# Values' product behind visit 2 of the feed-forward blocks; opening, passage to the experts and first late group in another order

## The chip, the cores and the metric

The kernel runs on one core of a Trainium2 chip. The metric is the device time of one execution in microseconds (us), the median of the runs. PE is TensorE, DVE VectorE, ACT ScalarE, POOL GpSimd and SP the sync engine, which here only issues DMAs. "Landing" is the moment at which the engine that waits for a DMA can go on.

## The reference

Input x has 16 sequences of 512 tokens, 128 features. First a linear attention block with a causal mask and no softmax, then a normed residual, then a mixture of 8 experts beside a shared feed-forward, and a second normed residual:

```python
q = silu(x @ Wq); k = silu(x @ Wk); v = x @ Wv          # 16 heads of 8
q = concat([q*cos(theta*n), q*sin(theta*n)]); k likewise
energy = einsum('bhnd,bhmd->bhnm', q, k) * tril
out = einsum('bhnm,bhmd->bhnd', energy, v) @ Wo * sigmoid(x @ G1 @ G2)
x = layernorm(x + (layernorm(out) * gamma + beta))
logits = rmsnorm(x) @ router_w.T        # two best of 8 experts, by capacity 1280
routed = scatter_add(expert(x[dispatch]) * w)
shared = silu(x @ sg) * (x @ su) @ sd
x = layernorm(x + shared + routed)
```

## The kernel before

Five engines have their own hand-written program, and semaphores alone tie them together; the order of the lines in each program is the order of execution.

**Stage 1** (up to 510 us) walks over the 16 sequences, "blocks" b = -1 to 17. Block b holds the core of attention for sequence b (PE's `energies`, `state`, `from_states`, `attend`, in four visits c = 0 to 3; DVE's `mask` and `mask_state`), the front of sequence b+1 (`project`, `values_projected`, `keys_turned`), and the back of the sequences before (norms, routing, `dispatch` by POOL). Blocks 2 to 11 (`with_feed_forward`) also run one shared feed-forward: eight pairs of `shared_gate(f)` and `shared_up(f)` on PE, `shared_silu` and `hidden_hi` on ACT, `shared_hidden` and `hidden_lo` on DVE. The gate's product and the energies share a bank of PSUM: `energies(c)` waits until ACT has read the gate before (`gates_before`), and `shared_gate(3)` waits until DVE has masked visit 2's first half of energies (`v_mask`). In the order of before, PE runs in the middle of such a block: out of visit 1, gate 2, `values_projected(0)`, up 2, energies of visit 2, gate 3. `values_projected(0)` is six matmuls (L2288 to L2290); ACT's `values` reads them out with three activations, and stands before `hidden_hi(b, 2)`.

**Opening** (0 to 20 us): POOL makes constants, SP loads `theta`, x and weights, DVE makes the angles of the rotary table in a chain of dependent small steps (L1183 to L1202), ACT takes their sine, DVE forms the table and turns the first queries and keys.

**Passage** (510 to 557 us): two further shared feed-forwards, called RELOADED and AGAIN (`spread_pair`, `spread_silu`, `spread_hidden`, `spread_down`), are woven with the norm and routing of the last two sequences. Each sequence's rows go to the experts' table in eight indirect DMAs issued by POOL (`dispatch`, L627); dispatch 16 needs the slots that DVE works out in `slots(B, 0)`, dispatch 17 those of `slots(B + 1, 1)`. When all have landed, SP loads the first expert's rows, and PE turns them (L2382).

**Stage 2** (557 to 755 us) walks over the 8 experts, PE without a wait; POOL adds their rows to the sums in DRAM.

**Stage 3** (755 to 823 us) adds three late feed-forwards (g = 0, 1, 2) to the sums and norms 16 sums ("jobs"; FIRST_JOB is 0, 3, 9, 15). A job is loaded into one of six buffers, DVE takes statistics (`stats`, `spread`), POOL the reciprocal root, ACT norms it in place (`normed`, 4 activations), SP stores it. SP's queue holds, for job n: wait for the norm, store job n, wait until that store has completed, load job n+6 into the same buffer. `added` puts the feed-forward's result, which stands in bank UB, onto its job; the next group's first up (L1850 on `bank`) writes UB and waits for it.

```python
need(sp, m_o, 4 * (n + 1) - (2 if g == LATE else 0))
sp.dma_start(out_v[m], ac[:, n % NB]).then_inc(m_st[n % NB], 16)
load_sums(n + NB)
```

## Time and profile before

| what | us |
|---|---|
| median of 3 runs (823.49 to 828.65) | 825.48 |
| the profiled execution's own time | 824.92 |
| its span, first to last instruction | 822.9 |
| PE busy | 768.0 (93%) |
| DVE busy | 586.1 (71%) |
| POOL busy | 405.8 (49%) |
| ACT busy | 368.4 (45%) |
| share of PE in the chain that ended last | 77% |

The profile is of one execution. PE's busy time is that of pipelined matmuls, so 93% does not say that PE is at its peak; it says that PE seldom stands still. In block 4 one matmul of 128x512 starts about 0.23 us after the one before while its record is 0.39 us long, so lengths of a stretch are read from starts. An "idle before" in brackets behind a row names the time for which the engine had nothing to do, and who ended it.

### The profile page before, as it was taken

The numbers are of one execution on the slowest core, as the hardware profiler recorded it, in microseconds if no ns is written. First come the engines' busy times: TensorE is split into PE (matmuls) and PEld (weight loads), VectorE is DVE, ScalarE is ACT, GpSimd is POOL, SyncE is SP. The second block draws the span as 40 slices with busy tenths as digits, with TensorE's granted clock in tenths as the row PEclk, the third lists the DMA queues.
The fourth block names the chain that finished last, engine by engine and source line by source line (L and its number), as shares of the span: only waits on it lengthen the run. The fifth ranks groups of instructions, "written<-read, shape, count | busy, mean of one in ns | idle before, by whom it ended". The sixth has DMA issues, their size and how long they took to land.

```text
span 822.9 us, 30732 instructions
## 1 busy us (share of the span) xinstructions
PE 768.0 (93%) x12462; PEld 625.8 (76%) x12462; DVE 586.1 (71%) x1866; ACT 368.4 (45%) x802; POOL 405.8 (49%) x395
## 2 busy tenths in 40 slices
PE   5889999999999999999998898989999999999994
PEld 3667777777777777777776676768999988899884
DVE  7488898888888898898878988744444454544675
ACT  6425554646556464554633331223323333323584
POOL 5541242523335243332534554571677778876442
PEclk9999999999999999999999999999999999999998
DMA  4155233231423323232222212113443445433555
GB/s 146 47 174 179 80 91 82 64 98 48 99 76 78 89 57 96 58 88 76 69 73 63 61 33 67 46 58 128 98 86 45 89 98 105 71 50 43 128 148 145
DMA packets 71164, 70.56 MB, mean 86 GB/s; under 512 B 11444, under 2 KB 54251, under 8 KB 71025
## 3 DMA queue, kind: packets, MB, share of 16 engines
q1 hardware_dynamic: 54000, 52.33, 23.0%
q0 software_dynamic: 17024, 16.28, 11.0%
q8 instruction: 99, 1.62, 0.9%
q14 instruction: 41, 0.33, 0.1%
HBM read 23.99 MB, written 28.89 MB: 64 GB/s over the span
## 4 chain that ended last, share of the span: by engine, by line
PE 77%; DVE 11%; issue 4%; DMA 3%; POOL 2%; SPq 1%; ACT 1%; POOLq 0%; ACTq 0%; DVEq 0%
PE energy_banks L1932 6%; PE bank L1850 5%; PE energy_and_gate_banks L1850 5%; PE bank L1852 5%; PE bank L1851 5%; PE bank L2406 4%; PE energy_and_gate_banks L2406 4%; PE energy_and_gate_banks L1957 4%; PE energy_and_gate_banks L1852 3%; PE energy_and_gate_banks L1851 3%; PE bank L1891 3%; DVE EM L1242 3%; PE energy_banks L1850 3%; PE energy_banks L1852 3%; PE energy_banks L1851 3%
## 5 line engine op out<-in xcount | busy, mean ns | idle before, releaser
L627 POOL DMA_INDIRECT dispatched_rows<-x,slot x128 | 130.5, 1019 | 236.4 <-PE energy_banks L1932 142.8
L761 POOL DMA_INDIRECT summed_rows<-VP,goal_i x80 | 123.8, 1548 | 43.3 <-issue 22.7
L1119 ACT ACTIVATE sq<-energy_banks 128x512 f32<-128x512 f32 (+1 forms) x96 | 50.6, 527 | 120.2 <-PE energy_banks L1852 116.6
L832 ACT ACTIVATE sf<-energy_and_gate_banks 128x512 f32<-128x512 f32 x88 | 52.4, 596 | 70.5 <-PE energy_and_gate_banks L1852 69.8
L842 ACT ACTIVATE hidden_rounded<-sf 128x512 fp32r<-128x512 f32 x88 | 55.3, 628 | 52.4 <-DVE sf L1272 52.4
L1272 DVE TENSOR_TENSOR sf<-sf,bank 128x512 f32<-128x512 f32 x88 | 60.3, 685 | 18.3 <-PE bank L1852 16.8
L1932 PE MATMUL energy_banks<-EM,VP 64*32 64x64 f32 x4096 | 59.0, 227 | 2.2 <-issue 2.2
L1850 PE MATMUL energy_and_gate_banks<-xgT_hi,ws_hi 128*128 128x512 f32 x108 | 51.7, 479 | 9.9 <-DVE EM L1242 9.3
L1242 DVE TENSOR_TENSOR EM<-energy_and_gate_banks,causal 128x512 f32<-128x512 f32 x64 | 44.1, 688 | 20.1 <-PE energy_banks L1957 20.0
L1932 PEld LDWEIGHTS energy_banks<-EM,VP 64*32 64x32 f32 x4096 | 47.6, 106 | 5.4 <-issue 4.6
L1850 PE MATMUL bank<-xgT_hi,ws_hi 128*128 128x512 f32 x108 | 45.5, 421 | 3.6 <-DVE QM L1789 1.7
L1724 DVE TENSOR_TENSOR he<-sq,bank 128x512 f32<-128x512 f32 (+1 forms) x48 | 28.8, 599 | 27.1 <-PE bank L1852 22.3
L1957 PE MATMUL energy_and_gate_banks<-QM,KT 32*64 32x128 f32 x1024 | 43.9, 281 | 2.9 <-issue 2.2
L1957 PEld LDWEIGHTS energy_and_gate_banks<-QM,KT 32*64 32x64 f32 x1024 | 28.6, 132 | 22.7 <-issue 22.4
L1957 PE MATMUL energy_banks<-QM,KT 32*64 32x128 f32 x1024 | 44.3, 282 | 0.9 <-issue 0.9
L1242 DVE TENSOR_TENSOR EM<-energy_banks,causal 128x512 f32<-128x512 f32 x64 | 43.5, 680 | 0.0
L1852 PE MATMUL bank<-xgT_hi,ws_lo 128*128 128x512 f32 x108 | 42.7, 395 | 0.0
L1852 PE MATMUL energy_and_gate_banks<-xgT_hi,ws_lo 128*128 128x512 f32 x108 | 42.7, 395 | 0.0
L1851 PE MATMUL bank<-xgT_lo,ws_hi 128*128 128x512 f32 x108 | 42.6, 395 | 0.0
L1851 PE MATMUL energy_and_gate_banks<-xgT_lo,ws_hi 128*128 128x512 f32 x108 | 42.5, 394 | 0.0
L1977 PE MATMUL bank<-VP,Kt 64*32 64x32 f32 x1792 | 40.6, 198 | 1.2 <-ACT Kt L891 0.8
L1724 DVE TENSOR_TENSOR he<-sq,energy_and_gate_banks 128x512 f32<-128x512 f32 (+1 forms) x48 | 28.8, 599 | 16.5 <-PE energy_and_gate_banks L1852 12.6
(256 smaller groups left out, 2189.4 us busy)
## 6 DMA issues: line engine op xcount, KB each, us to landing
QM<-QT SPq DMA_DIRECT2D x248, 32.0 KB
dispatched_rows<-empty POOLq DMA_DIRECT2D x8, 655.0 KB, 4.2
QM<-dispatched_rows SPq DMA_DIRECT2D x8, 655.0 KB, 5.6
QT<-sq SPq DMA_DIRECT2D x40, 128.0 KB, 2.8
KT<-sq SPq DMA_DIRECT2D x40, 128.0 KB
xin<-in_x SPq DMA_DIRECT2D x16, 256.0 KB, 2.9
QM<-summed_rows SPq DMA_DIRECT2D x16, 256.0 KB, 2.8
out_x<-QM SPq DMA_DIRECT2D x16, 256.0 KB, 3.2
```

The costliest lines, as they stand in the source:

```text
L627: g.indirect_dma_start(out=xg_d, out_offset=bass.IndirectOffsetOnAxis(ap=slot[:, n % 2, j:j + 1], axis=0), in_=x1[:, n % 2, j % NC, :], in ...
L761: g.indirect_dma_start(out=sum_d, out_offset=bass.IndirectOffsetOnAxis(ap=goal_i[:, par, t:t + 1], axis=0), in_=ye[:, par, t, :], in_offse ...
L842: a.activation(hs_hi[:, f], sf[:, n % SF], ACT.Copy).then_inc(a_hh, 1)
L1242: v.tensor_tensor(EM[:, c % 2, i].rearrange("p (r h) n -> p r h n", r=2), (EG2, EB2)[i][:, :, 0:4 * T].rearrange("p r (h n) -> p r h n", h=4),
L1272: v.tensor_tensor(sf[:, n % SF], sf[:, n % SF], UB[:], ALU.mult).then_inc(v_h, 1)
L1724: v.tensor_tensor(he[:, hp, f, 0:w], sq[:, f % 2, 0:w], EB[2 + f % 2][:, 0:w], ALU.mult).then_inc(e_h, 1)
L1850: t.matmul(dst, w_hi, x_hi, start=True, stop=False)
L1851: t.matmul(dst, w_hi, x_lo, start=False, stop=False)
L1852: return t.matmul(dst, w_lo, x_hi, start=False, stop=True)
L1932: ins = t.matmul(AV2[32 * j:32 * j + 32, s, cols], VP[keys, par, c, 32 * h:32 * h + 32], EM[keys, c % 2, h % 8 // 4, h % 4 // 2 * 4 + h // ...
L1957: ins = t.matmul((EG2, EB2)[r // 2][T * s:T * (s + 1), r % 2, 2 * T * t2:2 * T * (t2 + 1)], KT[rows, par, t2, P * c + T * s:P * c + T * (s ...
L2406: ins = t.matmul((OB, SBK)[hp][:, P * c:P * (c + 1)], he[:, hp, f, P * c:P * (c + 1)], wd[:, par, f], start=(f == 0), stop=(f == 3))
```

## The change

- **Blocks 2 to 11.** PE runs `values_projected(0)` behind up 2 and visit 2's energies instead of between gate 2 and up 2. ACT runs `hidden_hi(b, 2)` before `values(f, fp, 0)`.
- **Opening.** The second half of `theta` is loaded from ACT's queue instead of SP's; POOL makes `bits` before `ident`; `bits` holds 0.25 in place of 1.0, so that one reduction gives the phase, and a multiplication falls away; two memsets of DVE stand ahead of its wait for POOL.
- **Passage.** DVE: `add_input(B)`, `second_moments(B)`, `mean_square(B)`, `slots(B, 0)` and `scale_x1(B, 1)` stand earlier, `shared_add(RELOADED)` behind the routing of B+1. PE: `down_back` before `positions(B)`; `positions(B + 1)` and parts of `spread_down(RELOADED)` change places. ACT: the copy of x1T before that of `xhi`.
- **Stage 3.** The loads of sums go 0, 3, 1, 2, 4, 5 instead of 0 to 5. DVE runs `added` for job 3 right behind the statistics of job 0, not behind those of jobs 0, 1 and 2. ACT norms only job 0 in group 0; job 1 and job 2 are normed between the silus of group 1.

```diff
@@ -384,7 +384,6 @@
...
             sp.dma_start(theta_s[0::2], theta_v[0]).then_inc(ld_t, 16)
-            sp.dma_start(theta_s[1::2], theta_v[1]).then_inc(ld_t, 16)
             sp.dma_start(xin[:, 0], x_v[0]).then_inc(ld_x, 16)
...
@@ -509,7 +508,7 @@
...
             sp.wait_ge(e_sc[1], 16 * CT * E // 2)
-            for n in range(NB):
+            for n in (0, FIRST_JOB[1], 1, 2, 4, 5):
                 load_sums(n)
...
@@ -528,18 +527,18 @@
...
             g = nc.gpsimd
-            g.memset(ident[:], 0.0).then_inc(c_id, 1)
-            gp.wait_ge(c_id, 1)
-            g.affine_select(out=ident[:], in_=ident[:], compare_op=ALU.not_equal, fill=1.0, base=0,
-                            pattern=[[-1, P]], channel_multiplier=1).then_inc(c_id, 1)
             g.memset(zeros[:], 0.0).then_inc(c_pool, 1)
...
             for n in (0, P // 4):
-                g.affine_select(out=bits[:, n:n + P // 4], in_=bits[:, n:n + P // 4], compare_op=ALU.not_equal, fill=1.0, base=-2 * n,
+                g.affine_select(out=bits[:, n:n + P // 4], in_=bits[:, n:n + P // 4], compare_op=ALU.not_equal, fill=0.25, base=-2 * n,
                                 pattern=[[-2, P // 4]], channel_multiplier=1).then_inc(c_pool, 1)
+            g.memset(ident[:], 0.0).then_inc(c_id, 1)
+            gp.wait_ge(c_id, 1)
+            g.affine_select(out=ident[:], in_=ident[:], compare_op=ALU.not_equal, fill=1.0, base=0,
+                            pattern=[[-1, P]], channel_multiplier=1).then_inc(c_id, 1)
 
...
@@ -778,6 +777,7 @@
...
             a = nc.scalar
+            act.dma_start(theta_s[1::2], theta.rearrange("(h t d) i -> t h d i", t=2, d=HD)[1]).then_inc(ld_t, 16)
             act.wait_ge(c_pool, 1)
...
@@ -962,8 +962,8 @@
...
                     shared_silu(b, 2)
+                    hidden_hi(b, 2)
                     values(f, fp, 0)
-                    hidden_hi(b, 2)
                     shared_silu(b, 3)
...
@@ -1083,11 +1083,11 @@
...
             spread_silu(RELOADED, 7)
+            act.wait_ge(pe_x1T, B)
+            a.activation(x1T[:], PB[1][:], ACT.Copy).then_inc(a_x1T, 1)
             act.wait_ge(pe_again, 2)
...
             a.activation(xhi[:, 1], OB[:], ACT.Copy).then_inc(a_x1h, 1)
-            act.wait_ge(pe_x1T, B)
-            a.activation(x1T[:], PB[1][:], ACT.Copy).then_inc(a_x1T, 1)
             second_choice(B + 1, 1)
...
@@ -1155,15 +1155,17 @@
...
                     shared_silu(f)
-                    if g > 0 and f in (0, 1):
+                    if g == 1:
+                        normed(n - 2 + f // 2, (2 * (f % 2), 2 * (f % 2) + 1))
+                    if g > 1 and f in (0, 1):
                         normed(n - 1, (2 * f, 2 * f + 1))
-                    if g > 0 and f in (3, 4):
+                    if g > 1 and f in (3, 4):
                         normed(n, (2 * f - 6, 2 * f - 5))
-                    if g > 0 and f in (5, 6):
+                    if g > 1 and f in (5, 6):
                         normed(n + 1, (2 * f - 10, 2 * f - 9))
...
                     split_late(r + 1, g + 2)
-                for k in (range(n, n + 2) if g == 0 else range(n + 2, n + (5 if g < LATE - 1 else 6))):
+                for k in (range(n, n + 1) if g == 0 else range(n + 2, n + (5 if g < LATE - 1 else 6))):
                     normed(k)
...
@@ -1179,11 +1181,10 @@
...
                 dve.wait_ge(c_dve, n_c[0])
-            dve.wait_ge(c_pool, 5)
-            link(v.tensor_reduce(cosine[:], bits[:], AX.X, ALU.add))
-            link(v.tensor_scalar(phase[:], cosine[:], 0.25, None, ALU.mult))
             for i in (0, 1):
                 link(v.memset(shift_by[:, i], 0.25 * i))
+            dve.wait_ge(c_pool, 5)
+            link(v.tensor_reduce(phase[:], bits[:], AX.X, ALU.add))
             link(v.tensor_scalar(shift_by[:, :, 0:2 * COARSE], shift_by[:, :, 0:2 * COARSE], phase[:, 0:1], None, ALU.add))
...
@@ -1655,30 +1656,30 @@
...
             centre(B)
+            add_input(B)
             spread_hidden(RELOADED, 2)
+            second_moments(B)
             copy_logits(B)
             two_best(B)
-            add_input(B)
             spread_hidden(RELOADED, 3)
             choices(B, 0)
+            mean_square(B)
             spread_hidden(RELOADED, 4)
-            second_moments(B)
             spread_hidden(RELOADED, 5)
-            mean_square(B)
             read_positions(B)
+            slots(B, 0)
             spread_hidden(RELOADED, 6)
-            slots(B, 0)
+            scale_x1(B, 1)
             spread_hidden(RELOADED, 7)
-            scale_x1(B, 1)
             dve.wait_ge(m_x1[0], 16)
...
             two_best(B + 1)
-            shared_add(RELOADED, x1t[:, 1])
             choices(B + 1, 1)
...
             slots(B + 1, 1)
+            shared_add(RELOADED, x1t[:, 1])
             for f in range(8):
...
@@ -1819,7 +1820,7 @@
...
                     return
-                if g > 0:
+                if g > 1:
                     added(r - 1, n)
...
@@ -1837,6 +1838,8 @@
...
                     spread(k)
+                    if g == 0 and k == n:
+                        added(r, FIRST_JOB[1])
             stage3(dve, group)
...
@@ -2133,9 +2136,9 @@
...
                     shared_gate(2)
-                    values_projected(0)
                     shared_up(2)
                     energies_and_state(2)
+                    values_projected(0)
                     shared_pair(3)
...
@@ -2347,18 +2350,18 @@
...
             spread_pair(RELOADED, 5)
+            down_back(SPARE, PB[0])
             positions(B)
-            down_back(SPARE, PB[0])
             spread_pair(RELOADED, 6)
...
             turn_again(1, x1[:, 0])
-            spread_down(RELOADED, (0, 1))
             turn_x1(B + 1, 1)
-            spread_down(RELOADED, (2,))
+            spread_down(RELOADED, (0,))
             logits(B + 1)
-            spread_down(RELOADED, (3,))
+            spread_down(RELOADED, (1,))
+            positions(B + 1)
+            spread_down(RELOADED, (2, 3))
             spread_pair(AGAIN, 0)
-            positions(B + 1)
             for f in range(1, 8):
...
             spread_down(AGAIN, (0, 1))
```

## Rows read from the trace of the kernel before

**Rows 1.** PE's waits in the whole run: us in total, times, longest
```profile
PE energy_and_gate_banks L1850 <- DVE EM L1242: 9.3, 13, 1.4
```

**Rows 2.** Timeline, block 4, PE: start us, us, what, idle before
```profile
144.35 0.28 PE L2288 MATMUL bank<-we_hi,xgT_hi 128*128 128x256 f32 x1
...
145.06 0.39 PE L1850 MATMUL bank<-xgT_hi,ws_hi 128*128 128x512 f32 x1
...
145.84 0.33 PE L1957 MATMUL energy_and_gate_banks<-QM,KT 32*64 32x128 f32 x2
...
147.43 0.50 PE L1850 MATMUL energy_and_gate_banks<-xgT_hi,ws_hi 128*128 128x512 f32 x1 [0.63 <-DVE EM L1242]
```

**Rows 3.** Timeline, block 4, DVE
```profile
145.09 0.68 DVE L1223 TENSOR_TENSOR QT<-QT,table 128x512 f32<-128x512 f32 x1
...
146.02 0.69 DVE L1272 TENSOR_TENSOR sf<-sf,bank 128x512 f32<-128x512 f32 x1 [0.24 <-PE bank L1852]
...
146.68 0.69 DVE L1242 TENSOR_TENSOR EM<-energy_and_gate_banks,causal 128x512 f32<-128x512 f32 x1
...
147.29 0.68 DVE L1242 TENSOR_TENSOR EM<-energy_banks,causal 128x512 f32<-128x512 f32 x1
```

**Rows 4.** Timeline, block 4, ACT
```profile
144.55 0.60 ACT L832 ACTIVATE sf<-energy_and_gate_banks 128x512 f32<-128x512 f32 x1
...
146.74 0.63 ACT L842 ACTIVATE hidden_rounded<-sf 128x512 fp32r<-128x512 f32 x1 [0.77 <-DVE sf L1272]
...
148.43 0.60 ACT L832 ACTIVATE sf<-energy_and_gate_banks 128x512 f32<-128x512 f32 x1 [1.05 <-PE energy_and_gate_banks L1852]
```

**Rows 5.** Timeline of the opening, SP's queue and DVE
```profile
0.80 0.84 SPq L386 DMA_DIRECT2D theta_s<-in_theta  x1
...
1.70 0.64 SPq L387 DMA_DIRECT2D theta_s<-in_theta  x1
...
3.69 0.23 DVE L1190 TENSOR_SCALAR SM<-y,theta_s 128x16 f32<-128x16 f32 x1
```

**Rows 6.** Timeline of the passage, POOL
```profile
518.18 1.05 POOL L600 TENSOR_TENSOR rs<-ve,minus_half 128x4 f32<-128x4 f32 x1
...
529.75 1.03 POOL L627 DMA_INDIRECT dispatched_rows<-x,slot  x1 [1.07 <-DVE slot L1407]
...
532.98 0.97 POOL L627 DMA_INDIRECT dispatched_rows<-x,slot  x1 [2.20 <-issue]
```

**Rows 7.** Timeline of the passage, DVE
```profile
520.08 0.19 DVE L1360 COPY lg<-bank 128x32 f32<-128x32 f32 x1 [0.62 <-PE bank L2267]
```

**Rows 8.** Timeline of the passage, PE
```profile
556.99 1.97 PE L2382 MATMUL bank<-ident,QM 128*128 128x128 f32 x8 [4.75 <-DMA QM<-dispatched_rows]
```

**Rows 9.** Chain that ended last, inside the first expert
```profile
568.92 0.87 PE bank L2382 x8
```

**Rows 10.** Stretches: bounds, length, PE busy (instructions), PEclk, DMA share, GB/s
```profile
57.00:58.00 1.00, 0.00 (x0) 1.00 0.38 120
...
59.00:60.00 1.00, 0.92 (x59) 0.50 0.26 59
```

**Rows 11.** Timeline of the last stage, SP's queue
```profile
774.61 0.39 SPq L521 DMA_DIRECT2D out_x<-QM  x1
...
776.93 0.32 SPq L503 DMA_DIRECT2D QM<-summed_rows  x1
...
777.29 0.51 SPq L521 DMA_DIRECT2D out_x<-QM  x1
...
810.53 0.32 SPq L503 DMA_DIRECT2D QM<-summed_rows  x1
```

**Rows 12.** Timeline of the last stage, ACT
```profile
772.94 3.19 ACT L1145 ACTIVATE QM<-QM,shift,rs 128x128 f32<-128x128 f32 x8 [5.70 <-POOL shift L774]
```

**Rows 13.** Timeline of the last stage, DVE
```profile
771.41 0.86 DVE L1760 BATCH_NORM_STATS2 st<-QM 128x6 f32<-128x128 f32 x4
```

**Rows 14.** Timeline of the last stage, PE
```profile
775.36 0.47 PE L1850 MATMUL bank<-xgT_hi,ws_hi 128*128 128x512 f32 x1 [1.57 <-DVE QM L1789]
```

## The prediction

> **What bounds the kernel now.** I read the page first: PE is busy for 93% of the span and holds 77% of the chain that ended last, so what doesn't shorten PE's path, or the few stretches in which PE waits, brings nothing. Then PE's waits: the largest entry by far is the shared gate behind DVE's mask, 9.3 us in 13 places [rows 1]. Ten of the 13 are one per block 2 to 11. The timeline of block 4 shows the place: energies of visit 2 start at 145.84, gate 3 could follow the state's product but stands for 0.63 and starts at 147.43 [rows 2], once DVE has run the hidden product at 146.02 and the mask's first half at 146.68 [rows 3]. Then the three places outside the blocks where the chain leaves PE: the opening, a chain of small DVE steps behind the load of theta [rows 5]; the passage, where POOL issues dispatches one after another while PE ends up idle for 4.75 [rows 6, 8]; and the last stage, where SP's queue is a chain of its own: from 776.93 to 810.53 it loads nine times (jobs 7 to 15 after job 6) and each step is "store, wait for its completion, load": 33.6 / 9 = 3.73 us each [rows 11].
>
> **Blocks 2 to 11.** Nothing is added or removed, six matmuls move. Their length is 145.06 - 144.35 = 0.71 [rows 2]. Without them up 2 runs at 144.35 and visit 2's energies could start 0.71 earlier, at 145.13. They need the gate's bank, which ACT reads from 144.55 to 145.15 [rows 4]; with a hand-over of about 0.06 (an estimate: gate 3 starts 0.06 after the mask's record ends, 146.68 + 0.69 against 147.43) [rows 2, 3] they start at 145.21, so 0.08 of the move is lost here. The values then fill the place in which PE stood. DVE now decides. It began its turn at 145.09 and starts operations of this shape 0.61 apart when it has work (146.68 to 147.29), so the hidden product starts at 145.70 instead of 146.02, where it had waited 0.24 for up 2, and the mask at 146.31 instead of 146.68 [rows 3]. Its input, the energies, started 0.63 earlier, so is there. Gate 3 starts 0.37 earlier, at 147.06. PE is ready for it at 147.43 - 0.63 = 146.80 plus 0.08 and a refill of the pipeline behind the values, about 0.1 (estimate: a first matmul's record is 0.50, a following one's 0.39), thus 146.98 [rows 2, 3]: a rest of 0.1 remains. Bounds: at least DVE's idle of 0.24, at most the whole wait of 0.63. I take 0.37, **10 x 0.37 = 3.7 us**; the bounds are 2.4 and 6.3.
>
> What is queued behind: on ACT, `hidden_hi(2)` now stands before the three activations of `values`. Before, these ran between silu 2's end at 145.15 and 146.74 - 0.77 = 145.97, so 0.82 [rows 4]. Now PE's values end about 147.0 and ACT is free at 147.8. The next silu can start when gate 3 is done, 148.43 - 0.37 = 148.06. This cover is 0.25 per block; beyond it silu 3, then gate 4, come late. DVE's order is unchanged; POOL's dispatches hang on PE's counts and move with them; SP's queue isn't touched. The product's bank is needed again only when the keys are turned, eight microseconds later.
>
> **Opening.** The first angle step, at 3.69, needs both halves of theta [rows 5]. The second was issued at 1.70, behind the first at 0.80; from ACT's queue it goes out beside the first, 0.9 earlier. SP's later loads (x, wqk) also move up by the 0.64 which that issue took. The DVE steps before it shrink by a reduction-and-scale hand-over, and POOL starts `bits` earlier, so theta is what is late next. ACT's table load comes behind its DMA issue; it is covered, since ACT's next needed work is the copy of wqk. The steps behind it, 3.69 to the table, keep their lengths in the sum. Gain between 0.6 (only SP's issue time of 0.64 comes off) and 1.5 (the 0.9 and the 0.64 add up where x, too, is waited for). I take **0.9**.
>
> **Passage.** The end of POOL's queue counts: dispatch 16's first DMA starts at 529.75, released by the slots, the second at 532.98 after 2.20 without work, and 14 more behind it [rows 6]; the rows land for PE at 556.99 [rows 8]. Earlier slots move all of it. In DVE's order, three things change ahead of `slots(B, 0)`: hidden 6 steps behind it (0.61, as above [rows 3]); the idle of 0.62 in front of the logits' copy [rows 7] is filled by `add_input`; and `add_input` now waits for POOL's root, which ends at 518.18 + 1.05 = 519.23 [rows 6]. By DVE's order that wait opens about 0.4 us. Gain 0.61 + 0.62 - 0.4 = **0.8**; bounds 0 (the root comes later) and 1.2 (it costs nothing). Behind that wait stand hidden 2 and 3 and so PE's ups 4 and 5, about 1 us late; and `spread_down(RELOADED)` behind `positions(B + 1)` pushes PE's end another microsecond or so. That is covered by PE's idle of 4.75 [rows 8], of which I expect about 2 to be left. Without that cover each microsecond would count in full. Slots of B+1 get earlier and POOL reaches dispatch 17 late, so nothing is gained there.
>
> **The clock at the passage's end.** In this run the eight transposes at 556.99 take 1.97 [rows 8], the same eight inside the first expert 0.87 [rows 9], and two products of the shared down follow, also slow; PE had stood for 4.75 us before. If the clock stays at 2.4 GHz the transposes give 1.1, and the downs perhaps 0.7 (an estimate: the same stretch again over what is left of the slow time). But the granted clock also fell to 0.50, that is 1.2 GHz, around 59, after an idle of only some 2 us of which 57 to 58 is a part [rows 10]; so I don't count it. The Trainium skill ("TensorE: Matmul & The Clock Gate", section "Why this matters for your kernels") advises against long idle gaps between bursts of matmuls, and by it the shorter pause would keep the clock up; the trace agrees only for the long gap, and shows a short one that cost it too.
>
> **Stage 3.** The gain aimed at is PE's wait of 1.57 in front of the group's first up [rows 14]: `added` can now run when the down product is done: PE was ready for that up at 775.36 - 1.57 = 773.8, behind a gate of about 0.7, so at 773.1. But PE has no place in what ends last here; SP's chain has. Store 0 goes at 774.61, its completion allows load 6 at 776.93, 2.32 later, then store 1 at 777.29 [rows 11]. Before, ACT had normed jobs 0 and 1 in one run, 772.94 to 776.13, 3.19 for eight activations [rows 12], so store 1 was ready. Now ACT norms job 0, then waits for gate 0's silu; and job 1's statistics stand on DVE behind `added` (0.7), from about 773.8 instead of 771.41 [rows 13], 2.4 later. Its norm can begin about 2.4 behind 774.5, at 776.9, needs 1.6 plus a silu of 0.5 between its halves: done near 779.0. Store 1 goes 1.75 late. It then runs alone, without load 6 beside it; store 0, alone, took 2.32 against a usual step of 3.73 - 0.36 = 3.4, so some 0.8 to 1 comes back. The rest stays on the chain to load 15 at 810.53, nine steps on [rows 11]. Loss between 0 (ACT is quicker) and 2.0; I take **0.9**.
>
> **Sum.** -3.7 - 0.9 - 0.8 + 0.9 = -4.5 us. Against the profiled execution: 822.9 of span becomes 818.4, and with the 2.0 around it 820.4. That execution lies 0.56 under the median of the runs, 825.48, on which I put the forecast: **821.0 us**.
>
> **Rivals.**
> - *The wait goes whole.* DVE's hand-over proves quicker and all 0.63 goes in ten blocks: 10 x 0.26 = 2.6 more, 818.4. For it: only 0.24 of idle lies in front of DVE; against it: the same, since the turn at 145.09 isn't moved. Chance 0.12.
> - *The clock stays up at the experts' start*, by the mechanism above: a further 1.8, 819.2. Chance 0.17.
> - *The change does not do what it says in the blocks*: the wait moves from gate 3 to the energies, because silu 2 sits on their bank. Only opening, passage and stage 3 are left: -0.9 - 0.8 + 0.9, 824.7. Against it: silu 2 ends at 145.15, 0.02 after the energies' earliest new start [rows 2, 4]. Chance 0.12.
> - *Slower.* ACT's values come between gate 3 and silu 3: gate 4 waits for silu 3. It decides from 0.25 + 0.37 = 0.62 us of lateness per block; if PE's values and their copies run 0.8 late, the block grows by 0.18, ten times, and with the other -0.8 the time is 826.5. At 0.7 late it is level with before. Chance 0.07.
>
> The forecast itself has 0.52. The range takes in the 0.12 and 0.17 below and the 0.12 above, with bounds of the terms: 817.0 to 825.0. Measurements here tell about 1% from no change, 8.3 us, so faster by over 1% means under 817.2; only the whole wait together with the clock and the long opening step gets there: 0.08. Slower by over 1% needs several of these to go wrong at once: 0.03. Within: 0.89.
>
> **What would show it.** PE's wait for the mask at gate 3 should fall from 0.63 to 0.1 to 0.3 per block, the block's period by 0.37, and a wait of at most 0.1 appear before visit 2's energies. The first angle step should start near 2.8. Dispatch 16 should start 0.8 earlier relative to the last block, PE's pause before the first expert should be near 2. SP's store 1 should come 4 us or more behind store 0 (2.68 before), and the span from store 0 to the end should grow by about 0.9, though PE's wait of 1.57 is gone. The forecast is wrong if ACT's silu 3 starts behind `values` and not behind gate 3, if the block's period doesn't move, or if store 1 isn't late.

## The result

The changed kernel takes 820.52 us (median of 20 runs, 816.84 to 825.40); the kernel before, on the same chips, 826.62 us (20 runs, 823.16 to 830.30). The ratio is 0.9927, 95% interval 0.9908 to 0.9947, thus 6.0 us less (4.4 to 7.6). The forecast was 821.0 us in a range of 817.0 to 825.0, and "within 1%". The profiled execution of the changed kernel has a span of 819.0 us, 3.9 under that of before. Line numbers in it are those of before plus 3 on PE (the gate is L1853), plus 1 on DVE, minus 1 on POOL and SP.

| | before | after |
|---|---|---|
| median of the runs, us | 826.62 | 820.52 |
| span of the profiled execution, us | 822.9 | 819.0 |
| PE's wait at the gate for DVE's mask, us (times) | 9.3 (13) | 2.6 (3) |
| period of blocks 4 to 10 (logits to logits), us | 35.23 | 34.96 |
| PE's pause ahead of the experts, us | 4.75 | 2.49 |
| loads of the last stage, first to last, us | 43.18 | 43.02 |

PE's waits of the whole run (us in total, times, longest) have the line of [rows 1] no longer at their head:

```profile
PE energy_and_gate_banks L1853 <- DVE EM L1243: 2.6, 3, 1.4
...
PE energy_and_gate_banks L1960 <- ACT sf L832: 0.4, 1, 0.4
```

The ten waits in blocks 2 to 11 (1.00 us in block 2, 0.63 in the others) are gone; the three that are left stand behind the blocks with a feed-forward. The second line is new: visit 2's energies wait once, in block 2, for ACT to have read their bank.

Block 4 in the timelines of PE, DVE and ACT (start, us, what, idle before it), which answer to [rows 2, 3, 4]:

```profile
144.92 0.33 PE L1960 MATMUL energy_and_gate_banks<-QM,KT 32*64 32x128 f32 x2
...
145.80 0.39 PE L2291 MATMUL bank<-we_hi,xgT_hi 128*128 128x256 f32 x1
...
146.26 0.38 PE L2291 MATMUL bank<-we_hi,xgT_hi 128*128 128x256 f32 x1
...
146.72 0.45 PE L1853 MATMUL energy_and_gate_banks<-xgT_hi,ws_hi 128*128 128x512 f32 x1
...
147.24 0.39 PE L1855 MATMUL energy_and_gate_banks<-xgT_hi,ws_lo 128*128 128x512 f32 x1
...
145.34 0.68 DVE L1273 TENSOR_TENSOR sf<-sf,bank 128x512 f32<-128x512 f32 x1
145.94 0.68 DVE L1243 TENSOR_TENSOR EM<-energy_and_gate_banks,causal 128x512 f32<-128x512 f32 x1
...
144.18 0.60 ACT L832 ACTIVATE sf<-energy_and_gate_banks 128x512 f32<-128x512 f32 x1
146.05 0.63 ACT L842 ACTIVATE hidden_rounded<-sf 128x512 fp32r<-128x512 f32 x1 [1.28 <-DVE sf L1273]
146.92 0.45 ACT L819 ACTIVATE VP<-bank 128x128 f32<-128x128 f32 x2 [0.24 <-PE bank L2293]
147.25 0.39 ACT L823 ACTIVATE th<-bank 128x256 f32<-128x256 f32 x1
147.67 0.60 ACT L832 ACTIVATE sf<-energy_and_gate_banks 128x512 f32<-128x512 f32 x1
```

PE goes from the energies (144.92) through the state's product to the values (145.80) and the gate (146.72) without a wait. DVE has no idle ahead of the hidden product at 145.34. ACT's silu 3 (147.67) still starts when gate 3 is done, 0.04 behind the record of its last matmul (147.24 + 0.39). It was the same 0.04 in the kernel before, where that silu starts at 148.43 [rows 4]:

```profile
148.00 0.39 PE L1852 MATMUL energy_and_gate_banks<-xgT_hi,ws_lo 128*128 128x512 f32 x1
```

What is new is that the values' tanh now stands close ahead of it, so that the idle of 1.05 [rows 4] is used up. The values take 0.92 us (145.80 to 146.72) instead of 0.71 [rows 2]: their first matmul now has a record of 0.39, and so has the fourth.

The opening, ACT's queue and DVE, against [rows 5]. The first block is the changed kernel, the second the kernel before:

```profile
0.80 1.21 ACTq L780 DMA_DIRECT2D theta_s<-in_theta  x1
...
3.15 0.23 DVE L1191 TENSOR_SCALAR SM<-y,theta_s 128x16 f32<-128x16 f32 x1 [0.68 <-DMA theta_s<-in_theta]
...
5.37 1.15 DVE L1201 SCALAR_TENSOR_TENSOR SM<-SM 128x192 f32<-128x192 f32 x3
6.55 1.34 DVE L1202 SCALAR_TENSOR_TENSOR SM<-SM 128x192 f32<-128x192 f32 x1
```

```profile
3.34 0.28 DVE L1187 TENSOR_SCALAR SM<-SM,phase 128x64 f32<-128x64 f32 x1
...
6.03 2.24 DVE L1200 SCALAR_TENSOR_TENSOR SM<-SM 128x192 f32<-128x192 f32 x3
8.30 0.36 DVE L1201 SCALAR_TENSOR_TENSOR SM<-SM 128x192 f32<-128x192 f32 x1
```

The second half of theta is issued at once, but the issue takes 1.21 us on ACT's queue, and the first angle step starts 0.54 earlier, not 0.9. In the kernel before no engine waited for theta: the step at 3.69 followed DVE's own step at 3.34 without idle. In the changed kernel DVE is ready 0.68 us ahead of it, and theta ends last. Of the 0.54, 0.38 is left where the table is written (9.81 to 9.43). The five steps ahead of that take 3.48 us together here (1.15 for three, then 1.34 and 0.99) and 3.20 in the kernel before (2.24, 0.36 and 0.60); in both a long one runs beside POOL's `we_lo` (6.75 to 8.05 before, 6.34 to 7.67 after), only it is not the same step. That POOL's work lengthens it is not shown. And in block 2 nothing is left of the gain. DVE turns the queries there behind their transfer; the first line is the kernel before, the second the changed one:

```profile
72.08 0.69 DVE L1223 TENSOR_TENSOR QT<-QT,table 128x512 f32<-128x512 f32 x1 [0.43 <-DMA QT<-sq]
```

```profile
72.04 0.69 DVE L1224 TENSOR_TENSOR QT<-QT,table 128x512 f32<-128x512 f32 x1 [0.89 <-DMA QT<-sq]
```

The passage on POOL, DVE and PE, against [rows 6, 7, 8]:

```profile
515.69 1.53 POOL L599 TENSOR_TENSOR rs<-ve,minus_half 128x4 f32<-128x4 f32 x1
...
527.09 1.03 POOL L626 DMA_INDIRECT dispatched_rows<-x,slot  x1 [1.68 <-DVE slot L1408]
530.32 0.97 POOL L626 DMA_INDIRECT dispatched_rows<-x,slot  x1 [2.19 <-issue]
...
517.42 1.14 DVE L1338 SCALAR_TENSOR_TENSOR s<-wv,rs,xb 128x128 f32<-128x128 f32 x4 [1.10 <-POOL rs L599]
...
554.76 1.09 PE L2385 MATMUL bank<-ident,QM 128*128 128x128 f32 x8 [2.49 <-DMA QM<-dispatched_rows]
...
559.40 0.47 PE L1853 MATMUL energy_banks<-xgT_hi,we_hi 128*128 128x512 f32 x1
```

The wait of `add_input` for POOL's root is there (1.10 instead of the 0.4 of the forecast), the 2.19 us ahead of the second dispatch too. PE's pause is 2.49 instead of 4.75, and the eight turns of the first rows take 1.09 instead of 1.97.

The last stage, SP's queue, against [rows 11]:

```profile
770.90 0.39 SPq L520 DMA_DIRECT2D out_x<-QM  x1
773.93 0.32 SPq L502 DMA_DIRECT2D QM<-summed_rows  x1
775.15 0.39 SPq L520 DMA_DIRECT2D out_x<-QM  x1
777.56 0.32 SPq L502 DMA_DIRECT2D QM<-summed_rows  x1
...
806.68 0.32 SPq L502 DMA_DIRECT2D QM<-summed_rows  x1
```

Store 1 comes 4.25 us behind store 0 (2.68 before), as forecast. From store 0 to load 15 there are 35.78 us, against 810.53 - 774.61 = 35.92 before [rows 11]: the 0.9 did not come.

**How the runs scatter.** The runs of one kernel differ by up to 9 us, and the clock explains most of it. The granted clock falls from 1.0 to 0.50 (from 2.4 to 1.2 GHz), mostly for 3.4 us and for up to 13.7 us, at places that change from run to run. In the profile of before it fell at 58.5, 471.5 and 556.8, in that of after at 59.2, 421.0 and 444.9. In all 14 profiles there is one more fall behind PE's last matmul (816.2 in before, 810.2 in after), where PE has nothing left to slow down. Of 239 runs of these kernels the record lists span and mean clock: with one level for each kernel, the span is 5.3 us longer for each 0.01 of mean clock that is missing, and scatters by only 1.2 us around that. A fall ahead of the experts costs about 1.5 us (measured below), so that the ratios of the runs have intervals of 0.2 to 0.3%, as much as each part of this change brings. What a part did is therefore read from distances inside the traces, and the ratio stands beside it.

### The profile page after: what moved, and what is told of

It reads as the page before. It is cut to its first block, busy times and chain, and to the rows that moved or that the text cites. A ratio compares the mean times of both kernels' runs of the same rounds, so it can differ in the third digit from the quotient of the medians.

```text
span 819.0 us, 30731 instructions
## 1 busy us (share of the span) xinstructions
PE 771.5 (94%) x12462; PEld 627.2 (77%) x12462; DVE 583.9 (71%) x1865; ACT 368.2 (45%) x802; POOL 415.7 (51%) x395
## 3 DMA queue, kind: packets, MB, share of 16 engines
q0 software_dynamic: 17024, 16.28, 11.0%
## 4 chain that ended last, share of the span: by engine, by line
PE 78%; DVE 10%; issue 4%; DMA 3%; SPq 2%; POOL 2%; ACT 1%; POOLq 0%; DVEq 0%; ACTq 0%
PE energy_banks L1935 5%; PE bank L1853 5%; PE energy_and_gate_banks L1853 5%; PE bank L1855 5%; PE bank L1854 5%; PE energy_and_gate_banks L2409 4%; PE bank L2409 4%; PE energy_and_gate_banks L1960 4%; PE energy_and_gate_banks L1855 3%; PE energy_and_gate_banks L1854 3%; PE bank L1894 3%; PE energy_banks L1853 3%; PE energy_banks L1855 3%; PE energy_banks L1854 3%; PE bank L1895 2%
## 5 line engine op out<-in xcount | busy, mean ns | idle before, releaser
L626 POOL DMA_INDIRECT dispatched_rows<-x,slot x128 | 140.0, 1093 | 224.5 <-PE energy_banks L1935 132.4
L1935 PE MATMUL energy_banks<-EM,VP 64*32 64x64 f32 x4096 | 59.1, 225 | 1.1 <-issue 1.1
L1853 PE MATMUL energy_and_gate_banks<-xgT_hi,ws_hi 128*128 128x512 f32 x108 | 52.1, 482 | 3.4 <-DVE EM L1243 2.6
L1853 PE MATMUL bank<-xgT_hi,ws_hi 128*128 128x512 f32 x108 | 45.9, 425 | 3.7 <-DVE sf L1273 1.4
L1853 PE MATMUL bank<-xgT_hi,we_hi 128*128 128x512 f32 (+1 forms) x92 | 37.5, 408 | 3.7 <-DVE xgT_lo L1205 3.0
```

The lines of the kernel that those rows point to most:

```text
L626: g.indirect_dma_start(out=xg_d, out_offset=bass.IndirectOffsetOnAxis(ap=slot[:, n % 2, j:j + 1], axis=0), in_=x1[:, n % 2, j % NC, :], in ...
L1853: t.matmul(dst, w_hi, x_hi, start=True, stop=False)
L1935: ins = t.matmul(AV2[32 * j:32 * j + 32, s, cols], VP[keys, par, c, 32 * h:32 * h + 32], EM[keys, c % 2, h % 8 // 4, h % 4 // 2 * 4 + h // ...
```

## The experiments

Each part was first made alone on the kernel before. The distances used below are in us, from one profiled execution of each kernel. A: logits of block 4 to logits of block 11 (135.75 to 382.37 in before), over seven; the expectations count the logits from the first that is there, so what they call blocks 3 and 10 is this distance, their "block 0" is block 2 of the kernel (65.04), their "block 1" and "block 2" are blocks 3 and 4 where logits are meant. B: the third dispatch ahead of POOL's root to dispatch 16 (514.59 to 529.75 in before). C: PE's pause ahead of the first rows. D: start of the rows' turns to the first expert's gate. E: first to last load of the last stage.

| kernel | A | B | C | D | E |
|---|---|---|---|---|---|
| before | 35.23 | 15.16 | 4.75 | 6.19 | 43.18 |
| blocks alone | 34.96 | 15.17 | 4.76 | 6.12 | 42.87 |
| opening alone | 35.26 | 15.12 | 4.62 | 6.09 | 43.18 |
| passage alone | 35.26 | 14.54 | 2.52 | 6.27 | 43.19 |
| last stage alone | 35.25 | 15.17 | 4.73 | 6.91 | 43.37 |
| blocks, ACT's order old | 35.04 | 15.15 | 4.65 | 6.25 | 43.17 |
| blocks, ACT's values cut | 34.97 | 15.11 | 4.72 | 6.28 | 42.76 |
| after | 34.96 | 15.01 | 2.49 | 4.64 | 43.02 |
| after, stores late | 34.97 | 14.53 | 1.98 | 6.27 | 42.65 |
| after, matmuls at 35.0 | 34.98 | 15.29 | 1.05 | 4.64 | 43.42 |
| after, pause of block 2 filled | 34.99 | 14.52 | 1.86 | 4.64 | 42.91 |
| after, down ahead of the rows | 34.95 | 14.52 | 0.48 | 2.85 | 43.15 |
| after, three edits | 34.95 | 14.52 | 0.15 | 2.85 | 43.59 |
| before, experts' pause filled | 35.27 | 15.17 | 2.02 | 4.64 | 42.37 |

**Blocks alone.** The edit is that of the diff in `with_feed_forward` on PE and ACT.

```diff
                     shared_gate(2)
-                    values_projected(0)
                     shared_up(2)
                     energies_and_state(2)
+                    values_projected(0)
```

> The kernel before with the edit of the blocks alone: the values' six matmuls behind visit 2's energies on PE, and ACT's hidden_hi(2) ahead of its values. From the profile of after, the block's period between the logits of blocks 3 and 10 fell from 35.22 to 34.96 us. My theory: this comes from the edit, so the same period here, 34.96, and ten blocks give 10 x 0.27 = 2.7 us, a ratio of 0.9967 to before. The prediction's size, 0.37 per block, would be a period of 34.85, 3.7 us, 0.9955. Rival: the blocks also gain through what the passage does to the clock or to the queues, then the period would be above 35.0. The clock at the experts' start is not touched by the edit: PE's pause before the first expert stays near 4.75 us and a drop of the granted clock near 556 stays.

Ratio 0.9954 (0.9927 to 0.9980). A is 34.96, 0.27 under before, as in the changed kernel: the gain of the blocks comes from this edit and from nothing else. PE's costliest lines over the seven blocks from the logits of block 4, before and then blocks alone (busy us, mean ns of one | idle ahead of them, and what ended it):

```profile
L1850 PE MATMUL energy_and_gate_banks<-xgT_hi,ws_hi 128*128 128x512 f32 x56 | 27.6, 492 | 4.5 <-DVE EM L1242 4.4
L1932 PE MATMUL energy_banks<-EM,VP 64*32 64x64 f32 x1741 | 24.4, 226 | 0.0
```

```profile
L1850 PE MATMUL energy_and_gate_banks<-xgT_hi,ws_hi 128*128 128x512 f32 x56 | 27.5, 492 | 0.1
L1932 PE MATMUL energy_banks<-EM,VP 64*32 64x64 f32 x1799 | 25.8, 225 | 0.0
```

All 4.4 us of waiting (0.63 times seven) are gone, and 1.92 us (0.27 times seven) of time is gained; against the other kernels without the edit, whose A is 35.25 to 35.27, it is 0.29 to 0.31 a block. Relative to the logits ahead of it, on the mean over the seven blocks, gate 3 starts 0.39 earlier (11.66 to 11.28) and gate 4 0.38 earlier, which is the step of the forecast; the gate behind that is only 0.29 earlier (16.28 to 15.99), and so is the rest of the block. Between the two stands the attention product of 64 matmuls, which takes 0.88 in before and 0.97 here. That is nearly the whole of what is lost; why the product grows isn't shown.

At the same mean clock and on the same chip, the runs of this kernel are 3.1 us (2.2 to 4.0) shorter than those of before: the one part of the four that the runs alone show clear of the clock.

**Opening alone.** The four hunks of the diff that touch the first steps of SP, POOL, ACT and DVE; its core:

```diff
-            sp.dma_start(theta_s[1::2], theta_v[1]).then_inc(ld_t, 16)
...
+            act.dma_start(theta_s[1::2], theta.rearrange("(h t d) i -> t h d i", t=2, d=HD)[1]).then_inc(ld_t, 16)
```

> The kernel before with the edit of the opening alone. In the profile of after the first angle step starts at 3.15 instead of 3.69, the logits of block 0 start 0.50 earlier, but in block 2 DVE's turn of the keys starts at 72.04 behind the transfer of the queries, against 72.08 before. My theory: the gain is swallowed there: the same turn starts at 72.0 to 72.1 here, and what is left behind block 2 is 0 to 0.1 us, a ratio of 0.9999 to 1.0000. Rival one: it is the order of the values in block 2, not the transfer, which cost that block its gain; then 0.4 to 0.5 us stay to the end (0.9994). Rival two: the prediction's 0.9 us (0.9989). The ratio's interval is near 0.001 wide, so the logits' starts decide between the first two.

Ratio 1.0003 (0.9975 to 1.0030). The first logits come at 63.64, 1.4 earlier than in the profile of before. That does not say that the edit gave 1.4: two kernels without it have theirs at 63.68 and 63.50 (ACT's order put back, the experts' pause filled). In these three the clock had not fallen ahead of the logits, as it had in before. DVE then stands 1.90 us for the queries:

```profile
72.16 0.69 DVE L1222 TENSOR_TENSOR QT<-QT,table 128x512 f32<-128x512 f32 x1 [1.90 <-DMA QT<-sq]
```

In eight of the nine other profiles in which DVE waited for this transfer, kernels with and without the opening's edit, the turn starts between 71.8 and 72.4 (in the ninth, ACT's values cut, at 73.05). So what the opening gains is swallowed here, and the edit brings nothing that these runs can show.

**Passage alone.** The three hunks of ACT, DVE and PE at the end of stage 1; what counts for dispatch 16 is DVE's:

```diff
             centre(B)
+            add_input(B)
             spread_hidden(RELOADED, 2)
+            second_moments(B)
...
             read_positions(B)
+            slots(B, 0)
             spread_hidden(RELOADED, 6)
-            slots(B, 0)
```

> The kernel before with the edit of the passage alone. In the profile of after, dispatch 16 gained only 0.1 to 0.15 us relative to the start of the passage (0.8 had been predicted), since add_input waits 1.10 us for POOL's root. My theory: the same here, 0.1 to 0.2, but PE's pause before the first expert is about 2.5 us instead of 4.75, no drop of the granted clock follows, and the eight transposes of the first rows take about 1.1 us instead of 1.97: together 1.5 us, so the time falls by 1.6 us, ratio 0.998. Rival: the clock at that place has nothing to do with the pause (it hangs on the time since the last drop, or on chance); then this run has the drop still, and the gain is 0.1 to 0.2 us, ratio 1.000.

Ratio 0.9970 (0.9943 to 0.9998), 2.5 us, of which most comes with the clock: the mean clock of these runs is 0.9898 against 0.9865 for before on the same chip, and at the same clock 0.5 us is left, which 0.9 either way can't tell from nothing. B falls by 0.62, where I expected 0.1 to 0.2 by the profile of after. The difference is POOL's root: 1.07 us here and 1.53 in the profile of after, and `add_input` waits 0.59 here and 1.10 there. Among the seven profiles with the passage's edit, the five with a root of 1.05 to 1.07 have B at 14.52 to 14.54, the two with 1.53 and 1.54 have 15.01 and 15.29. So the forecast's 0.8 was 0.6, and the profile of after had shown less of it than there is. The clock did not behave as I had expected either: the pause is 2.52, but the clock fell at 560.7, 0.6 us into the turns, and D is 6.27, as with the long pause.

**Last stage alone.** The four hunks of SP, ACT and DVE in stage 3; DVE's:

```diff
                     stats(k)
                     spread(k)
+                    if g == 0 and k == n:
+                        added(r, FIRST_JOB[1])
```

> The kernel before with the edit of the last stage alone. In the profile of after, store 1 came 4.25 us behind store 0 instead of 2.68, but the chain to load 15 was 0.14 us shorter than before, because one later step of 4.4 us before was 3.6 there. My theory: that long step was no part of the edit, and a late store 1 is given back by store 0 being quick (its completion 3.0 behind it when alone, not 3.7): the net is 0 to 0.3 us of loss, ratio 1.0000 to 1.0004. Rival one, the prediction: a loss of 0.9 us, 1.0011. Rival two: the edit removes the long step (other order, other fetches) and gains 0.5 to 1 us, 0.9990; then load 15 is reached over 0.5 us earlier behind store 0 than in a run of before, and store 6 to load 12 takes 3.6 us.

Ratio 0.9990 (0.9965 to 1.0015). Store 1 comes 4.18 us behind store 0, load 7 is 6.89 behind store 0 where before had 5.86, so 1.0 late; and E is 43.37, 0.19 over before. Over all profiles E is 42.96 on average in the seven without this edit (42.37 to 43.19) and 43.16 in the seven with it (42.65 to 43.59). The loss is 0.2 us, less than E scatters. What gave the rest back in these two is above all the step from load 11 to load 12: 4.76 us in before, 4.15 and 4.17 in opening alone and passage alone, but 3.98 in after and 3.58 here. Over all 14 profiles this step takes 3.74 to 4.76 us in the seven in which two transfers of instructions fall into it, and 3.48 to 3.85 in the seven with one. Two fall into it in four of seven kernels without the edit and in three of seven with it, after among these, so that it is not the edit which moves the chain out of their way. What does hold over all profiles: the eight steps behind load 7 take 28.79 to 29.35 us with the edit and 29.18 to 30.06 without, 0.6 less on the mean. Why isn't shown.

**ACT's order, put back.** Blocks alone, but `hidden_hi(b, 2)` behind `values(f, fp, 0)` again on ACT.

```diff
                     shared_silu(b, 2)
-                    hidden_hi(b, 2)
                     values(f, fp, 0)
+                    hidden_hi(b, 2)
                     shared_silu(b, 3)
```

> The kernel before with half of the blocks' edit: PE's six matmuls of the values stand behind visit 2's energies, but ACT keeps its old order, so hidden_hi(2) stands behind the three activations of the values. In the run with both halves (e1_blocks), block 4 showed PE's values ending at about 147.14, ACT's three activations from 147.17 to 147.9, silu 3 at 148.00, and gate 4 at 148.65, 0.05 us behind silu 3's end. My theory: here hidden_hi(2), some 0.5 us on ACT's path, is pushed in front of silu 3, silu 3 and gate 4 come 0.5 us late, and the block's period between the logits of blocks 3 and 10 is 34.96 + 0.5 = about 35.45, worse than before's 35.22: the time is 2.3 us above before, ratio 1.003. Rival, the cover of the prediction (0.25 us of idle ahead of silu 3, and a decision point of 0.62 us): only 0.5 - 0.25 = 0.25 is lost, period 35.2, ratio 1.000.

Ratio 0.9965 (0.9940 to 0.9990). Gate 4 does wait for silu 3 now. Waits of PE between 100 and 385 us:

```profile
PE energy_and_gate_banks L1850 <- ACT sf L832: 2.1, 8, 0.4
```

ACT in block 4:

```profile
148.23 0.39 ACT L823 ACTIVATE th<-bank 128x256 f32<-128x256 f32 x1
148.50 0.65 ACT L842 ACTIVATE hidden_rounded<-sf 128x512 fp32r<-128x512 f32 x1
149.02 0.60 ACT L832 ACTIVATE sf<-energy_and_gate_banks 128x512 f32<-128x512 f32 x1
```

The wait is 0.26 per block (0.41 in block 4, where silu 3 comes 0.37 later behind the logits than with both halves), half of what I expected. It is what the rival says, 0.5 less a cover of 0.25: ACT starts its next operation 0.27 behind the start of the values' tanh, and in the changed kernel silu 3 starts 0.42 to 0.57 behind it, 0.50 on the mean. That leaves ACT a cover of 0.24. But A is 35.04, only 0.08 more than with both halves: gate 4 is 0.27 late on the mean, the gate behind it only 0.06. The half edit still gains 0.2 per block. So the slower rival was far away: lateness beyond the cover does reach gate 4, but most of it is taken back behind.

**ACT's values cut in two.** Blocks alone, each of the three activations in two of half the width; the tanh:

```diff
+                if i == 0 and 3 <= f <= 12:
+                    a.activation(dst[:, 0:1], src[:, 0:1], ACT.Tanh, scale=0.5)
+                    a.activation(dst[:, 1:2], src[:, 1:2], ACT.Tanh, scale=0.5).then_inc(a_th, 1)
+                    return
                 a.activation(dst, src, ACT.Tanh, scale=0.5).then_inc(a_th, 1)
```

> The kernel before with the edit of the blocks, and in blocks 2 to 11 ACT's three activations of the first half of the values (two copies, one tanh) are cut into six of half the width. Nothing else changes, so only ACT's time between the values and silu 3 grows, by an estimated 0.35 to 0.5 us (three more starts; two copies of 128x128 start 0.33 us before the tanh, about 0.16 apart). This doubles the cost on which the slower rival of the prediction hangs. My theory: ACT has no cover left (silu 3 at 148.00 in block 4 of e1_blocks, no idle ahead of it), and gate 4 follows silu 3's end, so the whole of it shows: period 35.35 to 35.45, ratio to before 1.001 to 1.002, which turns a gain of 0.27 per block into a small loss. Rival, the prediction's cover of 0.25 us: period 35.1 to 35.2, ratio 0.998 to 1.000.

Ratio 0.9941 (0.9919 to 0.9964), A 34.97. The edit costs ACT less than I had expected. The four halves of the copies take 0.43 us from the first start to the tanh, the two copies had taken 0.33; the halves of the tanh start 0.16 apart, where the whole one had taken 0.27 to the next start. So ACT's work grows by about 0.15 us (an estimate from these starts) and not by 0.35 to 0.5. That is inside the cover of 0.24: silu 3 starts 0.03 or 0.04 behind gate 3's last matmul in six of the seven blocks and 0.09 behind it in the seventh, and the period doesn't move. My theory, that ACT has no cover left, is refuted by it.

**Two stores of empty rows later.** On the changed kernel, in POOL's part of block 2:

```diff
                     need(gp, pe_E, 8 * b + 2)
-                    fill(4 * b - 4)
...
                     need(gp, pe_av, 4 * b + 2)
+                    if b == 2:
+                        fill(4 * b - 4)
+                        fill(4 * b - 3)
                     fill(4 * b - 2)
```

> The changed kernel, with two of POOL's eight stores of empty rows (655 KB each, issued at 63.76 and 65.02, beside the transfer of the queries for block 2) issued about 12 us later, behind visit 2's attention product. In the profile of the changed kernel DVE stood 0.89 us for that transfer, until 72.04, and the same turn started at 72.04 to 72.4 in four profiles, whether the opening ended early or late. My theory: the stores share the transfer engines with the queries and set that time; here the turn starts by 71.2 (when DVE is ready) and blocks 1 and 2 end 0.8 us earlier: logits of block 1 at 99.6 to 99.9 where the clock fell as in the profile of the changed kernel (100.41), ratio to before lower by 0.001 than the changed kernel's own 0.9927. Rival: the transfer is bound by its own small packets or by its own issue, the stores do not matter, and the turn starts at 72.0 again, no gain.

Ratio 0.9928 (0.9905 to 0.9951). The turn of the queries (in block 2, for block 3) starts without a wait:

```profile
70.37 0.68 DVE L1228 TENSOR_TENSOR QT<-QT,table 128x512 f32<-128x512 f32 x1
```

That is 1.7 us earlier than in after, though the clock fell at 59.1 as there (59.2), and the logits of block 4 come at 133.92, 1.46 earlier; 0.7 of this was there at the first logits already (63.84 against 64.54). Against the kernel with the pause of block 2 filled (below), which has its first logits at 63.86 and waits 1.8 for the queries, block 4's come 1.7 earlier (135.62 there). DMA between 63 and 72 us, after and then this kernel:

```profile
DMA packets 1622, 2.55 MB, mean 283 GB/s; under 512 B 155, under 2 KB 1179, under 8 KB 1619
dispatched_rows<-empty POOLq DMA_DIRECT2D x2, 655.0 KB
```

```profile
DMA packets 1441, 1.36 MB, mean 151 GB/s; under 512 B 156, under 2 KB 1180, under 8 KB 1438
```

The two stores were half of what the DMA engines moved while the queries were under way. This is shown for the transfer, by one profile against the ten that waited; why the first logits were already 0.7 earlier is not. The ratio of the runs, 0.9928 against the changed kernel's 0.9927, can't tell 1.7 us.

**Five matmuls, misplaced.** On the changed kernel, in `first_blocks`:

```diff
+                    if b == 1:
+                        for _ in range(5):
+                            t.matmul(UB[:], wqk_hi[:, 0:P], wqk_hi[:, 0:512], start=True, stop=True)
                     states_and_out(0)
```

> The changed kernel, with five matmuls of 512 columns (1.2 us, result unused) on PE behind the turn of the input in block 1, where PE pauses for 2 us (56.1 to 58.1 in the profile of before). The granted clock fell to 0.50 shortly behind that pause in four of six profiles (58.5, 59.2, 59.9 us; later, at 65.8 and 77.3, in two; in one it did not fall), for 3.4 to 13.7 us. My theory: the pause brings the clock down, and with it filled the clock stays at 1.0 until the blocks have passed; at 0.50 a stretch takes up to twice its time, so this saves 1.5 us for a drop of 3.4 us and more for a longer one: about 2 us on the median, ratio to before 0.990 to 0.991, and the highest of the runs come down. Rival: the clock falls for another reason (chance, or the load of the transfers), the drop is there at 58 to 60 all the same, and the ratio stays 0.993.

Ratio 0.9926 (0.9904 to 0.9948). They ran at 35.0, a block early, where PE has no pause, and the pause of 1.95 ahead of 58.12 was untouched. The clock fell at 46.1, 59.8 and 517.2. It tells nothing on the pause.

**Five matmuls in the pause of block 2.** The same in `with_feed_forward`:

```diff
                     if b == 2:
                         input_turned()
+                        for _ in range(5):
+                            t.matmul(UB[:], wqk_hi[:, 0:P], wqk_hi[:, 0:512], start=True, stop=True)
```

> The changed kernel with five matmuls of 512 columns, result unused, now in the pause itself: behind the turn of the input in block 2, ahead of a pause that lasted 1.2 to 2.0 us in eight profiles (56.1 to 58.1 in that of before). In e9_fill_pause the same five stood one block too early, at 35.0, where PE has no pause; they ran there for 1.0 us, and the clock still fell at 59.8. My theory: PE's pause of 2 us has to do with the fall of the clock at 58.5 to 59.9 (six of eight profiles without a fall at another place before it), and with 1.2 us of it filled no fall comes before 66: blocks 1 and 2 end 1.0 to 1.7 us earlier. Rival: the fall comes all the same between 58 and 60, so that the pause isn't the cause.

Ratio 0.9910 (0.9884 to 0.9937). The pause went from 2 to 0.53 us and the clock did not fall before 808, behind PE's last matmul; but in the next kernel, without the matmuls and with a pause of 1.72, it did not fall either, and in the one behind it, with them, it fell at 52.1 and 65.7. For pauses of this length the question stays open.

**A quarter of the shared down ahead of the first rows.** On the changed kernel:

```diff
-            spread_down(AGAIN, (0, 1))
+            spread_down(AGAIN, (0, 1, 2))
...
                     turn_rows(0, 0, (0, 1))
-                    spread_down(AGAIN, (2,))
-                    turn_rows(0, 0, (2,))
                     spread_down(AGAIN, (3,))
+                    turn_rows(0, 0, (2,))
```

> The changed kernel, with one product moved at the experts' start. In its profile PE pauses for 2.49 us for the first rows (until 554.76), turns them, and then runs a quarter of the shared down (16 matmuls, 1.8 us, 555.69 to 557.48) before the last turn, another quarter, and the first expert's gate at 559.40. Here that quarter stands ahead of the pause. My theory: it fills 1.8 of the 2.5 us with work that had stood behind, so the first expert's gate comes 1.7 to 1.8 us earlier behind the rows' turn (2.8 us instead of 4.64 behind its start), because DVE's and ACT's parts of the rows are done by 557.4, and the clock stays at 1.0 there; the time falls by 1.7 us against the changed kernel, ratio to before about 0.9905 against 0.9927. Rival: POOL's split of the weights or the transfer of the rows ends last, or the product in the pause comes late itself, and the gate starts at the same distance as before.

Ratio 0.9918 (0.9885 to 0.9950). D is 2.85 instead of 4.64, as expected; PE pauses for 0.48 us:

```profile
552.33 1.10 PE L2385 MATMUL bank<-ident,QM 128*128 128x128 f32 x8 [0.48 <-DMA QM<-dispatched_rows]
...
555.18 0.48 PE L1853 MATMUL energy_banks<-xgT_hi,we_hi 128*128 128x512 f32 x1
```

**All three.** The diffs of the stores, of the pause of block 2 and of the shared down together.

> The changed kernel with three edits together: the two late stores of empty rows of e7_fill_late (there the turn of the queries started at 70.4 instead of 72.04, and block 2's logits at 133.92 instead of 135.38), the quarter of the shared down ahead of the first rows of e8_down_first, and the five matmuls in the pause of block 2 of e10_fill_pause2. If each gives what its trace shows or should show, 1.5 and 1.7 and 1.0 us, the time is 4 us under the changed kernel's, ratio to before 0.988; if the matmuls in the pause give nothing, 0.989 to 0.990. Rival: what the early edits give is taken back by a transfer or by a fall of the clock later on, and the ratio is 0.992.

Ratio 0.9875 (0.9848 to 0.9902), median 816.31 us over 5 runs (814.94 to 817.21), 825.27 for before beside them. This is the fastest kernel of the study, by 0.5% under the changed one, and its interval lies wholly under the changed kernel's. D is 2.85 in it as well. Its turn of the queries starts at 73.1 without a wait for the transfer, behind two falls of the clock; its logits of block 4 come at 136.42, so that of the two early edits nothing is to be seen in this one profile, and the ratio stands on the runs.

**The experts' pause filled, on the kernel before.** The last run asks for the clock alone:

```diff
                 if e == 0:
+                    for _ in range(12):
+                        t.matmul(PB[1][:], ws_hi[:, 0, 0:P], ws_hi[:, 1, 0:512], start=True, stop=True)
                     turn_rows(0, 0, (0, 1))
```

> The kernel before, with twelve matmuls of 512 columns, result unused, at the start of PE's pause ahead of the experts' first rows. Six profiles had a pause of 4.62 to 4.76 us there, and in all six the granted clock fell to 0.50 at the end of it, the eight turns took 1.8 to 1.97 us and the first expert's gate came 6.1 to 6.9 us behind the start of the turns; of seven profiles with a pause of 0.15 to 2.52 us two had the fall. Nothing else moves: the twelve take about 2.9 us, the pause that is left is about 1.9. My theory: it is the pause that brings the clock down; here it stays at 1.0, the turns take 1.09 us and the gate comes 4.64 us behind their start, so the time falls by 1.5 us, ratio 0.998. Rival: the fall belongs to this place (the transfers, the load of code, the time since the last fall), then the turns take 1.97 us and the gate is 6.1 to 6.3 us behind them, ratio 1.000. The five matmuls in the pause of block 2 had left this open: the clock stayed up there in a run with the pause filled and in one without.

The twelve, the turns and the gate behind them, in this kernel's timeline of PE; [rows 8] has the turns in before:

```profile
550.45 2.98 PE L2411 MATMUL bank<-ws_hi 128*128 128x512 f32 x12
...
555.45 1.09 PE L2382 MATMUL bank<-ident,QM 128*128 128x128 f32 x8 [2.02 <-DMA QM<-dispatched_rows]
...
560.09 0.47 PE L1850 MATMUL energy_banks<-xgT_hi,we_hi 128*128 128x512 f32 x1
```

The pause is 2.02, the clock doesn't fall, the turns take 1.09 and D is 4.64 instead of 6.1 to 6.3: 1.5 us, by matmuls whose result nobody reads. The median is 823.29 against 823.71, ratio 0.9997 (0.9975 to 1.0019), which can't tell 1.5 us (0.0018) from nothing. Nor does the mean clock of the 12 runs rise: 0.9892 against 0.9889, where one fall of 3.4 us less in each run would be 0.002 and the standard error of the difference is 0.0013. Six of six profiles with a pause of 4.62 to 4.76 had the fall, this one, otherwise the same kernel, had not. That speaks for the pause as the cause, but it is one profile: with a pause of 0.15 to 2.52, of which the 2.02 here is one, two of eight had the fall, so that it may come or stay away behind a short pause too.

## Why the prediction was right, and where it was not

The time (821.0 against 820.52), the range and "within 1%" held. The terms did not all:

- **Blocks, -3.7 forecast, -2.8 measured** (A 34.95 to 34.99 against 35.23 to 35.27, ten blocks). The mechanism was right step by step: DVE's hand-over loses its idle of 0.24, and gate 3 comes 0.37 earlier on the mean of the seven blocks (11.66 to 11.30 behind the logits); the energies start when the gate's bank is free; PE isn't idle before gate 3, where I had left 0.1. The mis-sized step is the last, "the block's period by 0.37": it took the place of the gain for the gain. Behind gate 4 a quarter of it is lost again, in one longer attention product. The values' own length (0.92 instead of 0.71) did not matter, it fell into the wait.
- **ACT's cover of 0.25 us.** It is there, 0.24 on the mean, and the sign of being wrong that I had named did not show: silu 3 starts behind gate 3, by the same 0.04 as before, and not behind `values`. Work put on ACT inside the cover cost nothing (0.15, the cut activations), work beyond it made gate 4 wait (0.5, the old order: 0.26). What was too high is the price behind it, "beyond it silu 3, then gate 4, come late", taken one for one to the block's end: of the 0.26 only 0.08 per block was lost in the period. So the chance of 0.07 was if anything too large.
- **Opening, -0.9 forecast, 0 measured.** Two steps failed. "... from ACT's queue it goes out beside the first, 0.9 earlier" took the distance of two issues for the gain. In before theta was not what the first angle step waited for, DVE's own chain was; that chain got shorter, and theta, whose issue from ACT's queue took 1.21 us, now ends last, at 3.15: 0.54 earlier (0.33 in opening alone, 3.36). And that the steps "keep their lengths in the sum" holds only to block 2, where the transfer of the queries ends last, at 72.0 to 72.4. I had asked what is late next only for the angle steps, not for the blocks behind; the wait of 0.43 for the queries in the trace of before was there to be read.
- **Passage, -0.8 forecast, -0.6 measured** for dispatch 16 in five profiles of seven; in the two with the long root 0.15 was gained and 0.13 lost, so -0.45 on the mean. The mis-sized term is the wait of `add_input` for the root, 0.6 to 1.1 rather than 0.4.
- **The clock at the experts' start**, a rival at 0.17 and 1.8 us: it happened in the profile of after, and in five of the seven profiles that have the passage's edit. It is worth 1.5 us, so about 1.1 on the mean. I had weighed it by a short idle of 2 us that had brought the clock down in the opening; six falls behind six pauses of 4.62 to 4.76, against two in eight behind shorter ones, say that the length matters. The rule of the Trainium skill that I had set against it ("TensorE: Matmul & The Clock Gate", section "Why this matters for your kernels": no long idle gaps between bursts of matmuls) was the better guide here, though two pauses of 1.98 and 2.52 still had the fall.
- **Last stage, +0.9 forecast, +0.2 measured.** Store 1 was late by 1.5 to 1.6 (1.75 worked out), and load 7 by 0.8 to 1.0, which is the 0.9. The step that failed is "the rest stays on the chain to load 15": the eight steps behind it were together as much shorter (29.12 in after, 30.06 in before; 0.6 shorter on the mean of the profiles with the edit).

In sum -2.8 + 0 - 0.45 - 1.1 + 0.2 = -4.2 us by the traces, just short of the runs' interval of 4.4 to 7.6 less. The forecast of -4.5 was hit because the opening and part of the blocks that did not come were made up by the clock and by the last stage that did not lose. That the time was hit within 0.5 us is luck, twice over: errors of the terms cancel, and the forecast stood on three runs of before with a median of 825.48, where 20 runs have 826.62. The mean clocks of the single runs tell more than the traces here. At the same clock the changed kernel's span is 4.3 us under that of before (3.3 to 4.9, by the chip on which before ran). The terms without the clock's come to 3.05, so up to about 1.3 us of the 4.3 has no term that the traces show. The other 1.7 of the 6.0 lies in the clock, of which the 1.1 at the experts' start would be the larger part. How much of it is the change and how much is chance stays open, since the clocks of the runs of before beside the changed kernel aren't on record.
